# The last layer's rotation of queries and keys moved into the attention's block, with the values of two tiles between the permutation products and the first scores

## The reference

```python
def apply_rope(t):
    ...
    tp = t.reshape(*t.shape[:-1], d // 2, 2)
    t0, t1 = (tp[..., 0], tp[..., 1])
    rot = jnp.stack([t0 * cos - t1 * sin, t0 * sin + t1 * cos], axis=-1)
    return rot.reshape(t.shape)
...
q = apply_rope(q)
k = apply_rope(k)
q = q * (1.0 / jnp.sqrt(jnp.float32(hd)))
scores = jnp.einsum('bhqd,bhkd->bhqk', q, k)
attn = jax.nn.softmax(scores, axis=-1)
out = jnp.einsum('bhqk,bhkd->bhqd', attn, v)
```

## Time and profile before

| | |
|---|---|
| median of 3 runs | 3698.16 us (3697.8 to 3698.46) |
| the profiled execution | 3693.97 us |
| its span | 3692.3 us |
| PE, DVE, ACT, POOL busy | 3166.6, 1188.0, 688.8, 118.4 us |
| the rotation's block | about 2871.6 to 2887.4 us of the span |
| the attention's block | about 2887.4 to 3004.1 us of the span |

### The profile page before, as it was taken

One profiled execution on the slowest core, in us unless ns is written; L12 is line 12 of the kernel. 1 busy time (PEld: TensorE's weight loads), 2 busy tenths in 40 slices (PEclk: granted clock), 3 DMA queues, 4 the chain that ended last, 5 costly groups with the idle time before them and its releaser, 6 DMA issues. The chain is left out here.

```text
span 3692.3 us, 41285 instructions
## 1 busy us (share of the span) xinstructions
PE 3166.6 (86%) x16809; PEld 1544.7 (42%) x16809; DVE 1188.0 (32%) x2465; ACT 688.8 (19%) x1274; POOL 118.4 (3%) x150
## 2 busy tenths in 40 slices
PE   8998889996799799979778989899998897666666
PEld 4444543433344444344446666434445562111111
DVE  3555420001344569754423131203444411000000
ACT  2433101011233231110012121102433111000000
POOL 1000010001000000000000000000000100000000
PEclk9998889998899899989889999899998899777878
DMA  3100079996111021121332121792001237999998
GB/s 140 40 31 35 13 310 421 409 422 241 69 69 45 22 73 63 75 80 46 140 135 103 43 103 53 294 388 86 35 23 45 108 137 324 420 420 420 420 420 365
DMA packets 102711, 654.09 MB, mean 177 GB/s; under 512 B 18850, under 2 KB 28066, under 8 KB 39586
## 3 DMA queue, kind: packets, MB, share of 16 engines
q1 hardware_dynamic: 98402, 638.31, 42.9%
q0 software_dynamic: 4160, 13.63, 1.0%
HBM read 642.40 MB, written 9.50 MB: 177 GB/s over the span
## 5 line engine op out<-in xcount | busy, mean ns | idle before, releaser
L2725 PE MATMUL banks<-ring,h 128*32 128x512 f32 x1024 | 170.9, 784 | 71.0 <-DMA ring<-in_L_ffn_w 47.0
L773 PE MATMUL banks<-wvb,ctxT 128*128 128x512 f32 x512 | 231.0, 596 | 0.0
L2713 PE MATMUL banks<-ring,mine 128*32 128x512 f32 x1024 | 163.1, 701 | 69.2 <-DMA ring<-in_L_ffn_w 67.7
L1634 PE MATMUL banks<-ring,xT 128*64 128x512 f32 x736 | 167.9, 611 | 12.4 <-DMA ring<-in_L_ffn_Wg 5.6
L497 PE MATMUL banks<-normed_features,first 128*128 128x256 f32 x768 | 168.0, 380 | 1.1 <-ACT normed_features L463 1.1
L497 PEld LDWEIGHTS banks<-normed_features,first 128*128 128x128 f32 x768 | 144.7, 190 | 22.9 <-issue 3.2
L2814 DVE COPY mine<-mT 128x32 f32<-128x32 f32 x31 | 5.6, 181 | 449.2 <-PE banks L2713 449.2
L773 PEld LDWEIGHTS banks<-wvb,ctxT 128*128 128x128 f32 x512 | 92.9, 190 | 108.6 <-issue 106.1
L769 PE MATMUL banks<-extraT,wkb 128*128 128x512 f32 x256 | 116.1, 608 | 1.0 <-ACT extraT L879 1.0
L769 PE MATMUL banks<-ctxT,wkb 128*128 128x512 f32 x256 | 115.4, 596 | 1.4 <-PEq L141 1.4
L769 PE MATMUL banks<-ring 128*128 128x512 f32 x256 | 115.4, 596 | 1.4 <-PEq L141 1.4
(11 more groups left out here) (578 smaller groups left out, 4726.6 us busy)
## 6 DMA issues: line engine op xcount, KB each, us to landing
ring<-in_L_ffn_w SPq DMA_DIRECT2D x256, 1024.0 KB, 27.1
ring<-in_L_ffn_Wd SPq DMA_DIRECT2D x24, 2048.0 KB, 23.4
ring<-in_L_ffn_Wg SPq DMA_DIRECT2D x23, 2048.0 KB, 18.2
ring<-in_L_ffn_Wu SPq DMA_DIRECT2D x23, 2048.0 KB, 21.1
wb<-in_L_ffn_W SPq DMA_DIRECT2D x32, 1024.0 KB, 24.5
ctxT<-in_ctxT SPq DMA_DIRECT2D x16, 1024.0 KB, 4.9
first<-in_L_ffn_W SPq DMA_DIRECT2D x16, 1024.0 KB, 19.9
second<-in_L_ffn_W SPq DMA_DIRECT2D x16, 1024.0 KB, 22.0
```

The lines of the kernel that those rows point to most:

```text
L773: ins = pe.matmul(ps[:, u % 2, :], ctxT[:, par, k, r * P:(r + 1) * P], wvb[:, k, :], start=(k == 0), stop=(k == C - 1))
L1634: ins = pe.matmul(ps[H * side:H * side + H, 2 * kind + half, :], xT[:, p % 2, k, H * own:H * own + H], rows_of(where[(name, slot)], C)[:, ...
L2713: ins = pe.matmul(ps[B4 * q:B4 * q + B4, 0, :], mine[:, e % 2, k, :], w[:, q * 512:(q + 1) * 512], start=(k == 0), stop=(k == C - 1))
L2725: ins = pe.matmul(ps[B4 * q:B4 * q + B4, 2, :], h[:, Q * n + q, :], w[:, q * D:(q + 1) * D], start=(n == 0), stop=(n == Q - 1))
```

## The change

`rotate` is gone, and its work stands at the start of the attention's block. PE's permutation products use banks 0 to 3 in turn instead of eight banks, so from the fifth on each waits for a sine product. DVE's `tmp` has two pieces instead of eight (it lies in the scratch's `o`), and the addition of piece n - 1 follows the sine product of piece n. POOL has the cosine products ahead of its memset and copies. PE takes values(0) and values(1) between the last permutation product and scores(0), and values(2) ahead of scores(1). SP's loads of this block are issued at its start, which now lies ahead of the rotation.

```diff
 def attention(m, z, qT, kT, wv, wo, v_sent, out_sent, scale, vrow=None, orow=None, clip=None, bound=None, custom=False,
-              ahead=None, inside=None, norm=None, feats=None):
+              ahead=None, inside=None, norm=None, feats=None, rope=None):
...
+        if rope:
+            perm, trig, rope_sent = rope
+            turned_pairs, sin_s, cos_s, rotated = s("pairs_turned"), s("sin_multiplied"), s("cos_multiplied"), s("pairs_rotated")
+            over = lambda a: a.unsqueeze(1).to_broadcast([P, B, S])
+            by_batch = lambda a: a.rearrange("p (b s) -> p b s", b=B)
+            half_of = lambda n: (qT, kT)[n // C][:, n % C, :]
...
         @block.gpsimd
         def _(pool):
+            if rope:
+                for n in range(2 * C):
+                    pool.wait_ge(*turned_pairs.at(n + 1))
+                    pool.tensor_tensor(by_batch(half_of(n)), by_batch(half_of(n)), over(trig[:, 0, :]), ALU.mult)\
+                        .then_inc(*cos_s.up())
...
-            scores(0)
+            if rope:
+                pe.wait_ge(rope_sent.sem, rope_sent.made)
+                for n in range(2 * C):
+                    if n >= 4:
+                        pe.wait_ge(*sin_s.at(n - 3))
+                    pe.matmul(ps[:, n % 4, :], perm[:], half_of(n), start=True, stop=True).then_inc(*turned_pairs.up())
+            else:
+                scores(0)
             pe.wait_ge(v_sent.sem, v_sent.made)
             values(0)
             values(1)
+            if rope:
+                pe.wait_ge(*rotated.at(2 * C))
+                scores(0)
+                values(2)
             scores(1)
-            values(2)
+            if not rope:
+                values(2)
             turn_probs(0, 0)
...
+            if rope:
+                tmp = o[:].rearrange("p a n -> p (a n)").rearrange("p (a n) -> p a n", n=N)
+
+                def add_turned(n):
+                    dve.wait_ge(*sin_s.at(n + 1))
+                    dve.wait_ge(*cos_s.at(n + 1))
+                    dve.tensor_tensor(half_of(n), half_of(n), tmp[:, n % 2, :], ALU.add).then_inc(*rotated.up())
+
+                for n in range(2 * C):
+                    dve.wait_ge(*turned_pairs.at(n + 1))
+                    if n >= 2:
+                        dve.wait_ge(*rotated.at(n - 1))
+                    dve.tensor_tensor(by_batch(tmp[:, n % 2, :]), by_batch(ps[:, n % 4, :]), over(trig[:, 1, :]), ALU.mult)\
+                       .then_inc(*sin_s.up())
+                    if n:
+                        add_turned(n - 1)
+                add_turned(2 * C - 1)
...
-            rotate(m, q, k, perm, trig, small_sent, inside=slots(0, 2))
         second_sent = transformer_layer(m, z, n, names, ACT.Relu, q, k, qkh, wa, wb, wv, wo, cols, rows, b1c, small_sent, v_sent,
-                                        scratch=slots(0, 5), ahead=[gate_loads])
+                                        scratch=slots(0, 5), ahead=[gate_loads], rope=(perm, trig, small_sent))
```

More of the change, by code:

```diff
@@ L2183, in transformer_layer @@
 def transformer_layer(m, z, n, names, act, q, k, h, wa, wb, wv, wo, cols, rows, b1c, small_sent, v_sent, bound=None,
-                      scratch=None, ahead=()):
+                      scratch=None, ahead=(), rope=None):
     d = m.d
@@ L2193, in transformer_layer @@
     attention(m, z, q, k, wv, wo, v_sent, out_sent, 32 ** -0.5, rows[:, 0, :], rows[:, 1, :], bound=bound, inside=scratch,
-              norm=norm, feats=feats, ahead=[
+              norm=norm, feats=feats, rope=rope, ahead=[
                   (out_sent, (wo, d[names("wo")])), (ffn_sent, (wa, d[names("w1")])), (second_sent, (wb, d[names("w2")])),
@@ L2204, in small_loads @@
             (b1c, d[names("b1")])]
[L2207 to L2237, removed]
 def L2_attn(m, n, first, over_ctx, wv, wo, xattn_bv, xattn_sent, gw, gate_sent, disp, next_loads):
```

## The result

The changed kernel takes 3689.06 us (median of 17 runs, 3682.34 to 3699.49), the kernel before 3698.16 (17 runs, 3692.79 to 3709.9). The ratio is 0.9976, with a 95% interval of 0.9966 to 0.9986: 8.9 us less, 5.2 to 12.6. The prediction was 3689.4. A second set gave 3687.61 against 3697.22, ratio 0.9975 (0.9964 to 0.9987).

A forecast was written before the change was run, and what follows sets the result against it. The bound was a fixed-length stream of feed-forward weight transfers, started by the attention's end. Profiled 3693.97 less 8.7 us gives 3685.2; 4.2 more for the median gives 3689.4, with 8 in 10 between 3685.0 and 3694.0.

The forecast's parts named there:

- The gain is PE's idle time, filled: Between permutation products and scores(0), values fill PE's 8.67 us idle time; attend(0) at 26.2 us instead of 34.94.
- Turns at 1.68 us a pair: In the rotation, one DVE addition and one POOL cosine product take turns, together every 1.68 us.
- The rival without overlap: In the rotation, a pair costs 1.95 us; scores(0) at 17.2, total 3691.4 us; chance 7%.
- POOL keeping the turn: POOL's cosine products run back to back, addition 0 waits until 11.0 us; gain 2.7, total 3695.5 us; chance 6%.
- One sign: In the rotation on DVE, the additions would be mostly 1.2 to 1.75 us long.
- The low clock after idle time, 1.1 us: In scores(0) and the values on PE, 1.1 us of the gain is the low clock that idle time brought.
- The rest keeps its distances: Everything behind attend(0) keeps its distances, so the 8.7 us gain there reaches the end.
- the ring's first load: SP's first load of feed-forward weights after the attention, forecast 8.7 us earlier, near 2995.4 us.
- the rival of a shifted clock: In the attention's rounds, one more at low clock costs 2.7 us (12%); one or two fewer give 2.7 or 5.4 (13%).
- the 8.7 of the sum: Up to attend(0): 15.3 + 0.84 + 10.07 = 26.2 us against 34.94, 8.7 us less.
- 0.2%: For the whole kernel, 0.2%, 7.4 us, is about what a measurement can tell from no change.

The follow-up runs named there:

- e1: The changed kernel with scores(0) put back ahead of values(0) and values(1) on PE; 3695.2 us against 3695.77 for the kernel before.
- e4: The changed kernel with the sine products kept in PSUM, in six banks; 3681.99 us against 3695.77 for the kernel before, again 3686.14 against 3697.22.
- e2: As e1, but PE computes values(0) and values(1) once more, for nothing, ahead of scores(0); 3700.24 us (1 run) against 3695.77 for the kernel before.

## Why the prediction was right

- **The gain is PE's idle time, filled.** Right, and shown by e1: with the block fused and the old order on PE, attend(0) is at 34.55 and the ratio is 0.9996 (0.9984 to 1.0008); with the values moved, 26.14 and 0.9976 (0.9966 to 0.9986).
- **Turns at 1.68 us a pair.** Right in pace and at each place: last cosine product 13.74 (13.72), last addition 15.09 (15.2), scores(0) 15.14 (15.3), attend(0) 26.14 (26.2). e4 shows why they take turns. The rival without overlap, 17.2 at scores(0), and that of POOL keeping the turn, 21.3, did not come. One sign was wrong: the additions were forecast as mostly 1.2 to 1.75 long, and six of eight took 0.97. In the kernel before, an addition followed another at once and its length held its wait for the turn. With a sine product between them it starts later and waits less, at the same pace.
- **The low clock after idle time, 1.1 us.** Right in kind (e2), but it is no constant. In the second profile of before, values(0) and (1) took 9.61 us instead of 7.95, and attend(0) came at 36.59. From scores(0) to attend(0) the same work took 17.97 us in e2, at the full clock, and 19.16 and 20.81 in the two profiles of before. So the share of the clock in the gain at attend(0) is 1.2 to 2.8 us, and the whole gain there 8.8 to 10.4.
- **The rest keeps its distances.** Right within what the clock does: the ring's first load comes 9.8 to 10.6 us earlier over the two profiles of each kernel, 1 to 2 us more than forecast. From attend(0) to that load it is 97.6 and 96.2 us in the kernel before, 96.0 and 96.6 in the changed one; from attend(0) to attend(1) 13.2 and 12.1, then 11.7 and 12.3. Which rounds run at the low clock differs between profiles of one kernel, so the rival of a shifted clock is neither shown nor excluded for the last 1.5 us.
- **The number.** That 3689.4 met the median to 0.3 us is luck. The interval of the gain is 5.2 to 12.6 us, the second set gave 9.6, and the ring's load moved by more than the 8.7 of the sum.
- **What I took for granted.** That a measurement of this kernel tells 0.2% from no change rested on three runs within 0.7 us. The single runs scatter over 17 us, in both kernels; only medians of many, and the places, carry a difference of 9 us.

## What to carry to other kernels

When an engine waits at a block's end for a chain on others, look for work of its own that the chain doesn't feed, and put it there; here the order of four calls on PE was worth 8.4 us at attend(0), and the fusion that made it possible 0.4 by itself. Then look at what the chain does to itself: two engines that take turns show as lengths of 1.7 beside 1.3, and moving one input to PSUM freed them. Where the change is of the size of the scatter, measure distances between places in the trace, not spans, and take places near the change: the far ones carry the clock's changes.

## What the runs showed of the hardware

- DVE and POOL took turns here only when DVE had both inputs in SBUF: 1.72 us for a cosine product then, 1.28 with one of DVE's inputs in PSUM, with as many operations of the same size on both engines. POOL's small copies take part in it: 1.32 for two instead of 0.85.
- The stretch from the ring's first load to the end takes either 688 or 692 us in ten profiles (687.9 to 688.2 four times, 691.8 to 692.3 six times). The last eight records took 3.67 us each time in the first case and 5.9 to 6.5 in the second.
- Ahead of the changed place, the same code took 2871.6 to 2879.5 us in ten profiles. That is nearly as much scatter as the change is worth. The last stretch is not where it arises: from the block that PE starts near 2524 us to zero it is 351.2 to 351.4 us in all ten, while from the one that it starts near 1253 to that one it is 1267.4 to 1274.6. What differs inside that stretch was not followed.
